# Four transformer layers on one core: the next layer's first norm in halves of 512 tokens, and the second head group of wide cross attentions placed behind the first scores

## What is computed

```python
h = _ln(x) * (1 + scale) + shift          # adaptive norm, before every block
q, k, v = h @ Wq, h @ Wk, h @ Wv
x = x + softmax(q @ k.T * s) @ v @ Wo + bo          # self attention, 16 heads
h = _ln(x) * (1 + scale) + shift
x = x + softmax((h @ Wq) @ (ctx @ Wk).T * s) @ (ctx @ Wv) @ Wo + bo   # cross, 77 keys
h = _ln(x) * (1 + scale) + shift
x = x + gelu(h @ W1 + b1) @ W2 + b2       # layer 3: a * gelu(gate)
```

## Time and profile before

| | us |
|---|---|
| median of 3 runs (lowest, highest) | 4624.92 (4621.71, 4629.72) |
| the profiled execution, its own time | 4616.11 |
| its span | 4614.3 |
| TensorE matmuls busy | 4087.4 (89%) |
| VectorE busy | 3092.6 (67%) |
| ScalarE busy | 2080.6 (45%) |
| GpSimd busy | 1345.0 (29%) |
| mean granted TensorE clock | 0.95 |
| one gelu (L1523, L1526), one subtraction (L1911) alone | 0.69, 0.69 |

### The profile page before, as it was taken

One profiled execution on the slowest core, in us unless ns is written; L12 is line 12 of the kernel. 1 busy time (PEld: TensorE's weight loads), 2 busy tenths in 40 slices (PEclk: granted clock), 3 DMA queues, 4 the chain that ended last, 5 costly groups with the idle time before them and its releaser, 6 DMA issues.

```text
span 4614.3 us, 56558 instructions
## 1 busy us (share of the span) xinstructions
PE 4087.4 (89%) x20828; PEld 2506.3 (54%) x20828; DVE 3092.6 (67%) x4625; ACT 2080.6 (45%) x3756; POOL 1345.0 (29%) x664
## 2 busy tenths in 40 slices
PE   7999989789998887998999976878999999997889
PEld 5343356634334674555555545666555555546668
DVE  5888856688885655778777854444677677774355
ACT  2556644355554442444444435553344344444541
POOL 1100011100000123655565543421344444441120
PEclk8999989999998998999999988999999999998999
DMA  4223231123322232232223215423322222217420
GB/s 129 39 42 49 43 58 35 43 30 56 47 32 53 53 57 64 63 65 62 61 65 65 61 45 118 96 67 67 75 65 65 63 67 64 58 34 157 94 62 19
DMA packets 158516, 286.64 MB, mean 62 GB/s; under 512 B 36459, under 2 KB 70053, under 8 KB 157217
## 3 DMA queue, kind: packets, MB, share of 16 engines
q1 hardware_dynamic: 158240, 283.03, 29.5%
HBM read 105.01 MB, written 29.64 MB: 29 GB/s over the span
## 4 chain that ended last, share of the span: by engine, by line
PE 60%; DVE 16%; issue 6%; ACT 6%; POOL 5%; SPq 4%; DMA 3%; DVEq 0%; POOLq 0%; ACTq 0%
PE PS L979 25%; PE PS L1159 12%; PE PS L1055 4%; PE PS L1201 4%; PE PS L1051 4%; DVE t L1709 3%; PE PS L1289 3%; PE PS L1211 2%; DVE t L1705 2%; SPq L2154 2%; SPq L2137 2%; POOL t L1973 1%; DVE PS L1794 1%; POOL t L1999 1%; POOL t L1986 1%
## 5 line engine op out<-in xcount | busy, mean ns | idle before, releaser
L979 PE MATMUL PS<-t 128*128 128x512 f32 (+4 forms) x7896 | 1983.1, 382 | 153.5 <-ACT t L1423 30.6
L1423 ACT ACTIVATE t<-PS 128x512 f32<-128x512 f32 (+2 forms) x1600 | 1166.2, 750 | 1098.9 <-PE PS L979 1092.3
L979 PEld LDWEIGHTS PS<-t 128*128 128x128 f32 (+2 forms) x7896 | 1242.9, 186 | 700.6 <-issue 253.1
L1705 DVE TENSOR_REDUCE t<-PS 128x1 fp32r<-128x1024 f32 x512 | 621.6, 1219 | 285.8 <-PE PS L1051 278.9
L1159 PE MATMUL PS<-t 128*32 128x512 f32 (+2 forms) x4352 | 808.2, 609 | 0.2
L1709 DVE TENSOR_REDUCE t<-PS 128x1 f32<-128x512 f32 x1024 | 649.4, 683 | 71.7 <-PE PS L1055 70.3
L1999 POOL TENSOR_TENSOR t<-t 128x1024 f32<-128x1024 f32 x256 | 617.9, 2414 | 125.6 <-ACT t L1423 99.2
L1055 PE MATMUL PS<-t 96*128 96x512 bf16 x1024 | 371.4, 394 | 31.3 <-DVE t L1709 13.3
L1051 PE MATMUL PS<-t 128*128 128x512 f32 x1024 | 338.0, 413 | 63.4 <-DMA t<-t 35.9
L1995 POOL TENSOR_TENSOR t<-t 128x1024 f32<-128x1024 f32 x64 | 156.0, 2437 | 749.8 <-PE PS L1169 469.6
L1937 POOL TENSOR_TENSOR t<-t 128x2048 f32<-128x2048 f32 x24 | 109.6, 4566 | 830.5 <-DMA t<-in_rows 561.4
(11 more groups left out here) (134 smaller groups left out, 3959.7 us busy)
## 6 DMA issues: line engine op xcount, KB each, us to landing
t<-t SPq DMA_DIRECT2D x512, 128.0 KB, 3.4
t<-t SPq DMA_DIRECT2D x256, 256.0 KB, 3.9
t<-scr_n SPq DMA_DIRECT2D x288, 128.0 KB, 6.2
scr_n<-t SPq DMA_DIRECT2D x72, 256.0 KB, 2.2
t<-t SPq DMA_DIRECT2D x256, 64.0 KB, 2.0
t<-in_L_Wg SPq DMA_DIRECT2D x16, 768.0 KB, 4.6
t<-in_L_W SPq DMA_DIRECT2D x36, 256.0 KB, 3.3
t<-in_L_Wo SPq DMA_DIRECT2D x64, 128.0 KB, 2.6
```

The source lines that it names most:

```text
L979: ins = e.matmul(out, l, r, start=i == 0, stop=i == len(terms) - 1, tile_position=tp)
L1423: e.activation(dst, src, ACT.Exp, scale=S.L.scale).then_inc(*expd.inc((S.i, i)))
L1705: e.tensor_reduce(S.MT[m % 2][:, qt, j:j + 1], o, AX.X, ALU.max, negate=True).then_inc(*bank_free[k].nth(nth))
```

## The change

- A norm's `ln_rstd` becomes two steps: `ln_var` (eps on VectorE, root on ScalarE) and `ln_rstd` (the reciprocal), each for tiles `lo` to `hi`. In plans with `norm_steps` they are neighbours of each other, in the feed-forward the reciprocal comes half a place later.
- In the feed-forwards of layers 0 to 2 the next layer's norm of batch 0 is cut in two: tokens 0 to 511 from place 12.1, tokens 512 to 1023 from 17.65, with waits for the half of X and of H that each needs. The weight steps go from 17.1 and 18.7 to 10 and 13. The row bias goes from 24.05 to 23.05 (that of batch 1 from 12.9 to 14.9). The projections, the stacking and the max products of the next layer go forward: layer 0 from 25 to 28.8 (max products 29 to 33.4) to 22.2 to 25.6 (28 to 33.4), layer 1 from 24.6 to 32.6 to chains at 22, 24.4, 26.8 and 29.2, layer 2 from 24.6 to 32.6 to 17.2, 18.7, 23 and 24.5.
- In wide cross attentions group 1's load stands behind the first two `qstack`, its split at -0.84, its projection at -0.82 to 0.2. In layer 2 groups 2 to 7 and their stacks come 0.3 to 1.7 places later, and the norm of batch 1 lies at 6.5 to 9.9, between the chains of groups 3 and 4.

```diff
@@ -59,6 +59,7 @@
         self.before = None
+        self.cut = s == 0 and b == 0 and L.i > 0
@@ -582,7 +583,7 @@
     def norm_steps(p):
-        out = [("ln_stats", p, t) for t in range(8)] + [("ln_rstd", p)]
+        out = [("ln_stats", p, t) for t in range(8)] + [("ln_var", p, 0, 8), ("ln_rstd", p, 0, 8)]
@@ -708,7 +709,8 @@
     order.extend(("ln_stats", first, t) for t in range(8))
-    order.append(("ln_rstd", first))
+    order.append(("ln_var", first, 0, 8))
+    order.append(("ln_rstd", first, 0, 8))
@@ -781,19 +783,31 @@
                 if S.cross:
-                    plan.put(-9, -9, [("w_load", p, 1), ("qstack", S, 0), ("qstack", S, 1), ("w_split", p, 1, 1)]
-                             + nat64_steps(S, 1, 0))
+                    plan.put(-9, -9, [("qstack", S, 0), ("qstack", S, 1), ("w_load", p, 1)])
+                    plan.put(-0.84, 0, [("w_split", p, 1, 1)])
+                    if L.rope:
+                        nat64_chain(plan, S, 1, 0, (-0.82, -0.02), (0, 0.1, 0.3, 0.75, 0.85))
+                    else:
+                        plan.put(-0.8, 0.2, nat64_steps(S, 1, 0))
...
                         o, pg = 4 * g - 9, S.parts[g // 4]
-                        plan.put(o, o, [("w_load", pg, g % 4)])
-                        plan.put(o + 1.0, o + 1.0, [("w_split", pg, g % 4, int(g != 4))])
+                        load, split, *chain = ((0.9, 1.6, 1.75, 3.35), (4.5, 5.25, 5.35, 6.95), (8.2, 9.3, 10, 11.4),
+                                               (12.6, 13.3, 13.4, 15), (16.2, 16.9, 17, 18.6), (19.8, 20.5, 20.6, 22.2)
+                                               )[g - 2] if L.rope else (o, o + 1)
+                        plan.put(load, 0, [("w_load", pg, g % 4)])
+                        plan.put(split, 0, [("w_split", pg, g % 4, int(g != 4))])
                         if L.rope:
-                            nat64_chain(plan, S, g, 0, (o + 1.3, o + 2.9), (0, 0.15, 0.3, 0.95, 1.1))
+                            nat64_chain(plan, S, g, 0, chain, (0, 0.15, 0.3, 0.95, 1.1))
...
                     for pi in range(2, 16):
-                        plan.put(2 * pi - 4.5, 0, [("qstack", S, pi)])
-                    plan.put(6.75, 9.2, norm_steps(nxt))
+                        late = {4: 4.5, 6: 8.1, 8: 12.55, 10: 16.15, 12: 19.75} if L.rope else {}
+                        plan.put(late.get(pi, 2 * pi - 4.5) if pi > 3 else (0.9, 1.5)[pi - 2], 0, [("qstack", S, pi)])
+                    if L.rope:
+                        plan.put(6.5, 8, norm_steps(nxt)[:10])
+                        plan.put(8.1, 9.9, norm_steps(nxt)[10:])
+                    else:
+                        plan.put(6.75, 9.2, norm_steps(nxt))
@@ -838,26 +852,35 @@
                 if p:
-                    at, gap, pace = (17.65, 0.05, 1.2) if b else (0.9, 0.35, 2)
-                    for t in range(8):
-                        plan.put(at + gap * t, 0, [("ln_stats", p, t)])
-                    plan.put(at + 8 * gap, 0, [("ln_rstd", p)])
-                    at += 8 * gap + 1
-                    for q in range(4):
-                        for t in range(2):
-                            plan.put(at + pace * (q + t / 2), 0, [("ln_norm", p, 2 * q + t)])
-                        plan.put(at + pace * q + 0.5 * pace + 1.6, 0, [("ln_turn", p, q)])
-                        plan.put(at + pace * q + 0.5 * pace + 2.3, 0, [("ln_split", p, q)])
-                    plan.put(at + 4 * pace + 0.2, 0, [("ln_bias", p)])
+                    halves = ((0, 4, 12.1, 0.05, 1.0), (4, 8, 17.65, 0.05, 1.0)) if b else ((0, 8, 0.9, 0.35, 2),)
+                    for lo, hi, at, gap, pace in halves:
+                        for t in range(lo, hi):
+                            plan.put(at + gap * (t - lo), 0, [("ln_stats", p, t)])
+                        at += (hi - lo) * gap
+                        plan.put(at, 0, [("ln_var", p, lo, hi)])
+                        plan.put(at + 0.5, 0, [("ln_rstd", p, lo, hi)])
+                        at += 1
+                        for q in range(lo // 2, hi // 2):
+                            for t in range(2):
+                                plan.put(at + pace * t / 2, 0, [("ln_norm", p, 2 * q + t)])
+                            plan.put(at + 0.5 * pace + 1.2, 0, [("ln_turn", p, q)])
+                            plan.put(at + 0.5 * pace + 2, 0, [("ln_split", p, q)])
+                            at += pace
+                    plan.put(at + 2.2, 0, [("ln_bias", p)])
                     for i, step in enumerate(weight_steps(p) if b else []):
-                        plan.put(17.1 + 1.6 * i, 0, [step])
+                        plan.put(10 + 3 * i, 0, [step])
                     if b and L.i == 0:
-                        begin16_steps(p.stage, plan, 20, 25, 28.8, 29, 33.4)
+                        begin16_steps(p.stage, plan, 20, 22.2, 25.6, 28, 33.4)
...
                             plan.put(19, 0, [("rope_load", p.stage)])
-                        plan.put(24.6, 28.6, nat64_steps(p.stage, 0, 0))
-                        plan.put(28.6, 32.6, nat64_steps(p.stage, 0, 1))
+                        if p.L.rope:
+                            for qk in range(2):
+                                nat64_chain(plan, p.stage, 0, qk, (22 + 4.8 * qk, 24.4 + 4.8 * qk), (0, 0.4, 0.7, 1.9, 2.3))
+                        else:
+                            for half, at in enumerate((17.2, 23)):
+                                for qk in range(2):
+                                    plan.put(at + 1.5 * qk, 0, [("nat64", p.stage, 0, qk, half)])
@@ -915,10 +938,10 @@
 
-    def h_end(p):
+    def h_end(p, half):
...
         if p.s == 2:
-            return ("up", p.stage.i, p.b, 1, 7, 1 if p.L.i == 3 else 0)
+            return ("up", p.stage.i, p.b, half, 7, 1 if p.L.i == 3 else 0)
@@ -1348,10 +1371,10 @@
                                  ).then_inc(*bank_free[k].nth(nth))
-            elif what == "ln_rstd":
-                p, = a
-                w.wait_ge(ln_var, p.i)
-                e.activation(ln_rs[:, :], ln_sd[:, :], ACT.Sqrt).then_inc(*ln_root.inc(p.i))
+            elif what == "ln_var":
+                p, lo, hi = a
+                w.wait_ge(ln_var, (p.i, lo))
+                e.activation(ln_rs[:, lo:hi], ln_sd[:, lo:hi], ACT.Sqrt).then_inc(*ln_root.inc((p.i, lo)))
@@ -1569,7 +1592,7 @@
                 elif p.before.s == 2:
-                    w.wait_ge(x_added, (p.before.stage.i, 2 * p.b + 1, 3))
+                    w.wait_ge(x_added, (p.before.stage.i, 2 * p.b + int(t >= 4 or not p.cut), 3))
@@ -1581,18 +1604,20 @@
                 e.bn_aggr(ln_mv[:, t, :], ln_st[:, t, :]).then_inc(*ln_stat.inc((p.i, t, 1)))
+            elif what == "ln_var":
+                p, lo, hi = a
+                w.wait_ge(ln_stat, (p.i, hi - 1, 1))
+                e.tensor_scalar(ln_sd[:, lo:hi], ln_mv[:, lo:hi, 1], p.L.eps, None, ALU.add).then_inc(*ln_var.inc((p.i, lo)))
             elif what == "ln_rstd":
-                p, = a
-                w.wait_ge(ln_stat, (p.i, 7, 1))
-                e.tensor_scalar(ln_sd[:, :], ln_mv[:, :, 1], p.L.eps, None, ALU.add).then_inc(*ln_var.inc(p.i))
-                w.wait_ge(ln_root, p.i)
-                e.reciprocal(ln_sd[:, :], ln_rs[:, :]).then_inc(*ln_recip.inc(p.i))
+                p, lo, hi = a
+                w.wait_ge(ln_root, (p.i, lo))
+                e.reciprocal(ln_sd[:, lo:hi], ln_rs[:, lo:hi]).then_inc(*ln_recip.inc((p.i, lo)))
...
                     w.wait_ge(bank_full[k], nth)
-                w.wait_ge(ln_recip, p.i)
+                w.wait_ge(ln_recip, (p.i, 4 if p.cut and t >= 4 else 0))
@@ -1601,7 +1626,7 @@
                 if old:
-                    k, nth = where[h_end(old[-1])]
+                    k, nth = where[h_end(old[-1], q // 2)]
...
                 e.tensor_copy(p.H[0][:, :, ts], HF[:, :, :]).then_inc(*ln_high.inc((p.i, q)))

```

## The result

The changed kernel took 4696.16 us (median of 4 runs, 4691.92 to 4698.99), the kernel before in the same session 4627.15. The ratio is 1.015 (95% interval 1.0132 to 1.0168): **slower** by 69 us or 1.5%, where 42 less was forecast. The profiled execution took 4698.99 us (span 4697.2).

| stage | before | after | difference | forecast |
|---|---|---|---|---|
| feed-forward, layer 0 | 150.7 | 152.0 | +1.3 | -16 |
| feed-forward, layer 1 | 154.5 | 146.7 | -7.8 | -23 |
| feed-forward, layer 2 | 142.3 | 148.5 | +6.3 | -9 |
| (new work in the first halves of these) | | | in these | +3 |
| cross attention, layer 2 | 337.7 | 385.4 | **+47.7** | -7 |

The account below looks back on a forecast made before the run. TensorE, the busiest engine, was taken as the bound, with idle time to win in the feed-forwards' second halves and wide cross attentions. 16 + 23 + 9 - 3 - 10 + 7 = 42 off 4624.9 gave 4583 us, range 4557 to 4606.

Parts of the forecast that it names:

- the later groups: Layer 2's cross attention: groups 0.3 to 1.7 places later, two no longer just ahead of the multiply; +2, bounds -15 and +5.
- the new work of the first halves: First halves of the three feed-forwards: weight split, four stats and second root on the same engines; -3, bounds 0 and -9.
- the separate root steps: All norms: six more table loads, 7.7 us, hidden, and VectorE free during the root; taken as nothing, bounds -3 and +5.
- Cross attention of layer 2: Whole stage: start 0, later groups +2, second batch's norm kept off the chains +5; a gain of 7 us.
- a gain of 5 for the norm: Layer 2's cross attention: second batch's norm kept off the chains, where TensorE stood 6.00 us; +5, bounds 0 and +9.
- Cross attention of layer 3: Second group's weight load behind 16 stack DMAs, first turn of probabilities at about 4191; a loss of 10, bounds -14 and +2.
- Rival (c): Layer 2's cross attention: rotary chains at new places hold up the units' multiplies; slower, 67 us more, 4650; chance 0.03.
- Feed-forwards: Layers 0 to 2: tails win 16, 23 and 9 us, new work in the first halves costs 3.
- Rival (b): Tails of the three feed-forwards: GpSimd holds VectorE, 60% reaches TensorE, 22 us lost, 4605; chance 0.14.
- Layer 0's tail: Second half of layer 0's feed-forward: stops of 3.40 and 6.64 go, first max product at 872.8; 16 won, bounds 10 and 22.
- Layer 1's tail: Second half of layer 1's feed-forward: no stop above 3, last rotary subtraction before the last down block; 23 won, bounds 15 and 27.
- Layer 2's tail: Second half of layer 2's feed-forward: two double projections moved earlier, two stops of about 0.6 left; 9 won, bounds 5 and 12.

Follow-up runs that it names:

- e1: The changed kernel with five weight loads of the wide cross attentions requested just ahead of the stacked queries' DMAs instead of behind them: median 4650.78 us, ratio 1.0059.
- e13: The kernel before with only the weight loads of the wide cross attentions made late, behind the stack DMAs: median 4692.56 us, ratio 1.0143.
- e10: The kernel before with the change's feed-forward part alone and GpSimd's row bias there cut to one tile of 32 columns, the other additions left out: ratio 0.9949.
- e6: The kernel before with the change's feed-forward part alone, GpSimd's row bias and weight split taken apart: 4618.88 us, ratio 0.9996.

## Why the prediction was wrong

Two steps failed. In layer 2's cross attention the later groups were put down as a gain of 2; the loads late in SyncE's queue and the new places made the stage lose 48. In the feed-forwards the new work of the first halves was put down as -3, bounds 0 and -9, and these parts lost 35, as much as all the rest won. A third term, the separate root steps, was taken as nothing and cost about 11.

**Cross attention of layer 2.** The prediction saw the mechanism, priced it for layer 3 and for the first load of layer 2, and both came out: the first turns were 11.5 us later in layer 3 (11 forecast) and 2.8 in layer 2 (1, taken as 0). But of the later groups it said that they "come 0.3 to 1.7 places later", a gain of 2 (bounds -15 and +5). The load order of groups 4 to 7, where the stack stands 0.05 to 0.1 of a place *ahead* of the load, was not read out of the diff; before, the load stood half a place ahead. Each makes the load late by what SyncE needs for 8 DMAs, 7.3 us, and most of that reaches TensorE: 28 us in all by e1, of which 18.5 are idle time and 9.8 the slower clock, and 55 in the old plan by e13. Of the 48 DMAs that the loads of this stage were moved past, 16 had been counted. The rest, 19 us, is the new places of chains and norm, which were forecast as a gain of 5 for the norm: at the tenth unit e1 is 10.3 us ahead of the kernel before, but only because the fourth group's projections are still to come; at the 13th it is 1.3 behind.

**Cross attention of layer 3.** Right: +9.2 for +10. The terms were off by less than 2 us each and in part cancelled: the load landed sooner (3.7 us from issue to cast, 5.0 forecast), and what follows up to the first turn took longer (10.2 for 8.2).

**Rival (c)** gave the sign, but 25 of the 69 us (4650), and not the reason: TensorE's wait for the multiply fell to 35.7 us. It had a chance of 0.03, and no rival at all had the queue in layer 2.

**Feed-forwards.** Of 45 us forecast, less than 1 came: behind the boundary 35.4 of 48 were won, ahead of it 35.1 were lost. "TensorE stood nowhere long there" holds for layer 0, idle 1.1 of 51.8 us. It does not for layer 2, where TensorE already stood 6.86 and 4.72 us behind GpSimd. And it says where TensorE stood, not what was left to it: in layer 0 three things of the change now fall together, and each had been costed by itself. Bias and weight split stand side by side (8.3 us), and the root, "hidden", in fact held ScalarE for 5.5. "Hidden: two gelus take about 1.4 of each 2.82" compares sums, not the delay of the one gelu that TensorE waits for. The bias is 4 us of this by e10; how root, weight split and norm steps share the remainder is not separated.

**Rival (b)** had the mechanism and the place, and nearly the size: it counted 22 us in the tails, and e10 shows 16 behind the boundary. Its chance was 0.14, and its time, 4605, missed for what it took over from the forecast. The Trainium skill (SBUF — State Buffer, SBUF: two separate sides) has this contention as a lock held for the whole instruction; the trace agrees, 4.58 and 4.94 against 4.94 and 4.62 of GpSimd's.

**Layer 0's tail** won 13.3 of the 16 behind the boundary. But the forecast of 872.8 for the first max product, 20 us earlier than before, left TensorE no idle time: it was busy 99.25 of the 118.0 us up to there, so about 19 could be had. "TensorE is at place 28 at about 866" is 91.2 us after the stage's start, less than the 97.0 that TensorE is busy up to that product in e10. After the change the product came 118.7 us after the start, 0.7 later than before. The best kernel that leaves nothing out won 5 for the stage.

**Layer 1's tail** won 14.5 of 23. The stop of 8.52 shrank to 4.29 and moved ahead of the boundary, but two of 4.73 and 3.80 came behind the gelus' subtractions and the residual add, where none over 3 had been forecast. The last rotary subtraction came 143.9 us into the stage, where 124.3 (1723) was forecast: with the last down block, not before it. With GpSimd's instructions apart (e6) or short (e10) the stage won 16 and 18 of the 23.

**Layer 2's tail** won 7.6 of 9, with 14 matmuls of the projections moved ahead of the boundary. Of the "two stops of about 0.6" behind the split one was 0.64 and the other 3.51, and the 12 matmuls behind that took 5.44 us. On VectorE the last two splits stand behind a gelu subtraction that met the row bias. In e10, where that bias is short, the subtraction took 0.69 and the stop was 1.13 (last row):

```profile
3231.09 4.62 POOL L1962 TENSOR_TENSOR t<-t 128x2048 f32<-128x2048 f32 x1 [13.42 <-DVE t L1621]
3233.19 3.07 DVE L1936 TENSOR_TENSOR t<-t 128x512 fp32r<-128x512 f32 x1 [2.24 <-ACT t L1549]
...
3241.38 5.44 PE L1002 MATMUL PS<-t 128*128 128x512 f32 x12 [3.51 <-DVE t L1634]
```

```profile
3164.98 3.02 PE L991 MATMUL PS<-t 128*128 128x512 f32 x12 [1.13 <-DVE t L1623]
```

The stage's +6.3 is the highest of seven kernels with this plan (142.5 to 148.5, on average 144.5); the old plan gave 139.2 to 142.6, on average 140.9. So the halves cost this stage about 4 us, against 9 won by forecast.

**Roots.** Taken as nothing. The table loads were as forecast, 1.28 us each and 27 for 24 at the norm's line, and the next activation starts with the load's end (820.46 + 1.28 to 821.75 above). The Trainium skill's 2.66 us for a switch (ScalarE: Activation LUTs, What ACT_TABLE_LOAD costs) is not seen in these rows:

```profile
L1377 ACT ACT_TABLE_LOAD x27 | 34.6, 1283 | 0.5
```

What cost was, in layer 0, the wait between the two loads, and elsewhere the place: 27 steps instead of 26 on the same stretch, some 11 us in the two self attentions, for a part of the diff that looked like a renaming. The attention of layers 0 and 1 took 7 us more in sum after the change; a kernel without the two steps took longer still there (e10: 733.4 and 680.0), so the cause of this is not shown.
